# Where the rounded half of an FFN hidden block is read from, and which semaphore TensorE waits on for its bank

## The chip, the cores and the metric

The kernel runs on 1 core of a Trainium2 chip. The metric is device time of one execution in microseconds (us). Three runs of the kernel before took 3048.17, 3043.27 and 3048.67 us; their median is 3048.17 us.

## The reference

The reference is a stack of four residual sublayers over 32 independent sequences of 512 rows and 256 columns, all in fp32:

```
x = x + attn_a(layernorm(x))   # 16 heads, linear attention: phi = elu + 1, causal cumulative sums, numer / denom
x = x + ffn(layernorm(x))
x = x + attn_b(layernorm(x))   # 16 query heads on 4 kv heads, rotary, window of 64, softmax, pair mixing
x = x + ffn(layernorm(x))

def ffn(x):                    # W1: 1024 x 256, W2: 256 x 1024, both rounded to -1, 0, 1
    h = relu(x @ quantize(W1).T + b1)
    return h @ quantize(W2).T + b2
```

The change touches only the line of `h`.

## The kernel before

**Split numbers.** TensorE multiplies fp32r operands, which hold fewer bits than fp32. So each fp32 operand is kept as two fp32r halves: the rounded value and what is left over. For the FFN's hidden block these are `f_hh` (rounded, written by ScalarE) and `f_hl` (`f_r - f_hh`, written by VectorE, line 1314), where `f_r` is the relu in full fp32.

**One FFN turn.** A turn is one FFN over one sequence (512 rows): 8 blocks (`fb` 0 to 7) of 128 hidden units. `up(fb)` is four matmuls into a PSUM bank `HID` (line 439). ScalarE's `f_relu` (lines 969 to 976) reads that bank twice: once for `f_r`, once more for `f_hh`. VectorE's `low(fb)` makes `f_hl`. `down(fb)` adds eight matmuls into the banks `Y` (line 459). In the main loop all blocks use the one bank `HID[0]` (`ONE_HID`), so `up(fb+1)` has to wait until ScalarE is through with block `fb`.

**The order.** The order of work is written out by hand, one list for each engine. A step of the main loop has two phases. In phase 1 sequence `a` is in attention A, and an FFN of two other sequences is woven in; in phase 2 sequence `b` (the one before) is in attention B, again with FFN blocks between. Each phase runs blocks 5, 6, 7 of a carried turn and 0 to 4 of its own. So a step has 16 `f_relu`, one after another on ScalarE and in a fixed place of its queue. Each engine works through its own queue in order and waits on semaphores. All of this is unrolled in the program as `phase1` and `phase2` of each engine, and the middle steps are a hardware loop.

**Names that the prediction uses.** Start of phase 2 on TensorE: `up(5)`, `up(6)`, `down(4)`, `turn_q(0)` (line 744, waits for VectorE's `stack_lo(0)`, lines 1613 and 1614). On ScalarE: `relu(5)`, `raw(2)` (lines 1010, 1011, 1014), `stack_hi(0)` (lines 1133, 1134), `relu(6)`, `exps(0)` (line 1156). On VectorE, from the end of phase 1: `residual(3)` (line 1458), the roots (lines 1560 to 1583, each instruction waits for the one before by a semaphore of VectorE's own), `rotate` (line 1599), `stack_lo(0)`. On GpSimd: `sines` (lines 1805, 1806), released by `raw`. Later in phase 1: ScalarE's `relu(3)`, then `y_hi(2)` (line 1070), VectorE's `y_lo(2)` (line 1450), TensorE's `project(2)` (line 379). From phase 2 into phase 1: ScalarE's `relu(4)`, then `qk_exp(0)` (lines 1056, 1057); TensorE's `qk(2)` (line 379) waits for it. The start and the end of the program run an FFN by itself (`alone`).

**Semaphores.** `f_rr` counts finished `f_r`; `f_act` counts finished `f_hh`. Before the change nothing waits on `f_rr`.

Of the kernel before, what the change touches and what calls it, by code (L numbers as in the profile page):

```python
# [20 lines left out]
ACT = mybir.ActivationFunctionType  # L21
# [14 lines left out]
FB = FF // P  # L36
# [10 lines left out]
UPS, DOWNS = 5, 4  # L47
# [43 lines left out]
def needed(value):  # L91

    return not isinstance(value, int) or value > 0


def build(nc, x, w_qkv, w_out, w_b, wo_b, gain, mix, w1, b1, w2, b2, const, out):
    with ExitStack() as ctx:
        def sb(name, shape, dt=F32):
            return ctx.enter_context(nc.sbuf_tensor(name, shape, dt))

        def sem(name):
            return ctx.enter_context(nc.semaphore(name))
# [18 lines left out]
        b1c = sb("b1c", [P, FB])  # L121
# [15 lines left out]
        class Norm:  # L137
# [20 lines left out]
        f_r = sb("f_r", [P, 2, S])  # L158
        f_hh = sb("f_hh", [P, 2, S], F32R)
# [63 lines left out]
        f_h, f_rr, f_act, f_lo, f_w2, f_out = (sem(n) for n in (  # L223
            "f_hidden_ready", "f_relu_ready", "f_hi_ready", "f_lo_ready", "f_down_done", "f_added"))
# [46 lines left out]
        def first_turn(s):  # L271

            return None if s is None else 0 if isinstance(s, int) and s == 0 else s * 2 - 1

        def second_turn(s):

            return None if s is None else 2 * NSEQ - 1 if isinstance(s, int) and s == NSEQ - 1 else s * 2 + 2
# [85 lines left out]
        def _(pe):  # L363
# [19 lines left out]
            def norm_half(n, turn, hf, bank):  # L383
                pe.wait_ge(n.normed, turn * NT + 2 * hf + 2)
                for k in range(KB):
                    for t in range(2):
                        mm = pe.transpose(bank[:, k * D + t * P:k * D + (t + 1) * P],
                                          n.xn[:, 2 * hf + t, k * P:(k + 1) * P], ident)
                mm.then_inc(n.turned, 1)

            def norm_transpose(n, turn, banks):
                for hf in range(2):
                    norm_half(n, turn, hf, banks[hf])

            def at_half(turn, hf, own, carry):

                if turn is None:
                    return
                if hf:
                    pe.wait_ge(at.lo, turn * 2 + 1)  # L400
                elif own is not None:
                    pe.wait_ge(f_act, own * FB + 3)
                else:
                    pe.wait_ge(f_act, (carry + 1) * FB)
                norm_half(at, turn, hf, HID[0])

            def f_norm(turn):
                if needed(turn * FB):

                    pe.wait_ge(f_act, turn * FB)  # L410
                norm_transpose(ff, turn, HID)

            def f_half(turn, hf):

                if turn is None:
                    return
                if hf:
                    pe.wait_ge(ff.lo, turn * 2 + 1)
                elif needed(turn * FB):
                    pe.wait_ge(f_act, turn * FB)  # L420
                norm_half(ff, turn, hf, HID[0])

            def f_up(turn, fb, at_turn=None, banks=TWO_HID):

                if turn is None:
                    return
                if fb == 0:
                    pe.wait_ge(ff.lo, turn * 2 + 2)
                if fb == (UPS - 2 if banks is ONE_HID else UPS - 1) and at_turn is not None:

                    pe.wait_ge(at.lo, at_turn * 2 + 2)
                if banks is ONE_HID:
                    if fb:
                        pe.wait_ge(f_act, turn * FB + fb)
                elif fb >= 2:
                    pe.wait_ge(f_act, turn * FB + fb - 1)
                for k in range(KB):
                    for j, src in enumerate((ff.xh, ff.xl)):
                        mm = pe.matmul(banks[fb % 2][:], w1t[:, k, fb * P:(fb + 1) * P], src[:, k, :],  # L439
                                       start=(k == 0 and j == 0), stop=(k == KB - 1 and j == 1))  # L440
                mm.then_inc(f_h, 1)
# [22 lines left out]
            def f_unit(turn, k):  # L464
                if turn is not None:
                    if k + 1 < FB:
                        f_up(turn, k + 1)
                    if k >= 0:
                        f_down(turn, k)
# [5 lines left out]
            def alone(own, carry, last):  # L475

                for k in range(FB - DOWNS):
                    carried(carry, k)
                if own is not None:
                    f_norm(own)  # L480
                    for k in range(-1, FB if last else DOWNS):
                        f_unit(own, k)
# [39 lines left out]
            def program(guarded):  # L522
                def phase1(s):
                    a, n, own, carry = s.a, first_turn(s.a), second_turn(s.c), first_turn(s.b)
# [5 lines left out]
                    def up(fb):  # L530
                        f_up(own if fb < UPS else carry, fb, turn_b, ONE_HID)
# [4 lines left out]
                    def own_norm():  # L536
                        if own is not None:
                            f_norm(own)

                    def next_norm(half):  # L540
                        at_half(turn_b, half, own, carry)
# [25 lines left out]
                    def scores(ch):  # L567

                        if ch == 0:
                            pe.wait_ge(a_qz_s, (a + 1) * 4)  # L570
                            pe.wait_ge(a_ph, (a + 1) * 4)
                            pe.wait_ge(a_kt_s, (a + 1) * 2)
                            if own is not None:

                                pe.wait_ge(ff.lo, own * 2 + 2)
                            elif carry is not None:
                                pe.wait_ge(f_act, carry * FB + UPS)
                        else:

                            pe.wait_ge(a_sm, a * 16 + 4 * ch)  # L580
                            pe.wait_ge(a_ne, a * NT + ch)
                        for k in range(KB):
                            for r in range(4):
                                rows = slice(32 * r, 32 * r + 32)
                                mm = pe.matmul(A_SCORES[r][:, k * 2 * P:(k + 1) * 2 * P].rearrange("p (e q) -> p e q", e=2),  # L585
                                               a_kT[rows, k, ch * P:(ch + 1) * P], a_qz[rows, k, :, ch * P:(ch + 1) * P],
                                               start=(k == 0), stop=(k == KB - 1), skip_group_check=True)
                                if k == KB - 1:

                                    mm.then_inc(a_sc[r], 1)  # L590
# [78 lines left out]
                    down(6)  # L669
                    state(0)  # L670
                    scores(0)
                    up(0)
                    state(1)
# [4 lines left out]
                    up(1)  # L678
                    turn_numer(0)
                    scores(1)  # L680
                    up(2)
                    turn_y(0)
# [3 lines left out]
                    numer(1, 1)  # L686
                    turn_numer(1)
                    scores(2)
                    turn_y(1)
                    next_norm(0)  # L690
# [23 lines left out]
                def phase2(s):  # L714
# [5 lines left out]
                    def up(fb):  # L720
                        f_up(own if fb < UPS else carry, fb, turn_a, ONE_HID)
# [4 lines left out]
                    def own_norm(half):  # L726
                        f_half(own, half)

                    def next_norm(half):
                        at_half(turn_a, half, own, carry)  # L730
# [212 lines left out]
        def _(act):  # L943
# [25 lines left out]
            def f_relu(turn, fb, banks=TWO_HID):  # L969
                act.wait_ge(f_h, turn * FB + fb + 1)  # L970
                if needed(turn * FB + fb - 1):

                    act.wait_ge(f_lo, turn * FB + fb - 1)
                    act.wait_ge(f_w2, turn * FB + fb - 1)
                act.activation(f_r[:, fb % 2, :], banks[fb % 2][:], ACT.Relu, bias=b1c[:, fb:fb + 1]).then_inc(f_rr, 1)  # L975
                act.activation(f_hh[:, fb % 2, :], banks[fb % 2][:], ACT.Relu, bias=b1c[:, fb:fb + 1]).then_inc(f_act, 1)  # L976

            def alone(own, carry, last):
                if carry is not None:
                    for k in range(UPS, FB):  # L980
                        f_relu(carry, k)
                if own is not None:
                    f_norm(own)
                    for k in range(FB if last else UPS):
                        f_relu(own, k)
# [889 lines left out]
```

## Time and profile before

| | |
|---|---|
| median of 3 runs | 3048.17 us (3043.27 to 3048.67) |
| the profiled execution | 3042.93 us, its span 3041.1 us |
| TensorE busy | 2793.4 us, 92% of the span |
| VectorE busy | 2309.7 us, 76% |
| ScalarE busy | 1724.2 us, 57% |
| GpSimd busy | 475.7 us, 16% |
| mean granted TensorE clock | 0.986 of full speed |

In the rows further down, PE is TensorE's matmul row, PEld its weight loads, DVE VectorE, ACT ScalarE, POOL GpSimd. A timeline row begins with the start in us from the span's start and the duration in us. A duration reaches to the end of the instruction's last write; the next instruction of the same engine can start before that, so the spacing of two starts is shorter than a duration. Idle time of the engine just before an instruction stands in square brackets with what ended it; idle time under about 0.15 us is not printed. The share of busy time is an average over all stages.

### The profile page before, as it was taken

Reading aid. Unit: us, or ns where it says so; the run is one execution under the profiler, and the core shown is the slowest. Engines: PE = TensorE matmul, PEld = TensorE weight load, DVE = VectorE, ACT = ScalarE, POOL = GpSimd, SP = SyncE. Lnnn points to the kernel's source line nnn. Section 1 sums busy time; section 2 is a strip of 40 time slices with the busy share of each in tenths; the row PEclk is TensorE's granted clock in tenths of the full one; section 3 lists DMA queues with packets and bytes.
Section 4 is the critical chain, followed back from the end, with each engine's and each line's share of the span. In section 5 each row is a group of like instructions: output and inputs, shape, how many; then the busy total and the mean of one; then the engine's idle time right before and its main releaser. Section 6 shows DMA issues by size and latency. Waiting matters only on the chain. (4 is left out here: it accounts for less than half of the span.)

```text
span 3041.1 us, 75562 instructions
## 1 busy us (share of the span) xinstructions
PE 2793.4 (92%) x25924; PEld 2258.8 (74%) x25924; DVE 2309.7 (76%) x5982; ACT 1724.2 (57%) x3589; POOL 475.7 (16%) x1047
## 2 busy tenths in 40 slices
PE   5799999999999999999999999999999999999976
PEld 4577777777777777777777777777777777777764
DVE  6677787777788777788777788777788777788754
ACT  2356555566555566555566555566555556555554
POOL 4111111111111111111111111111111111111110
PEclk8999999999999999999999999999999999999998
DMA  2000000000000000000000000000000000000000
GB/s 69 8 11 17 16 16 3 14 16 16 16 16 3 14 16 16 16 16 7 9 16 16 16 16 9 7 16 16 16 16 10 6 16 16 16 16 11 6 11 17
DMA packets 42114, 45.10 MB, mean 15 GB/s; under 512 B 2640, under 2 KB 41424, under 8 KB 42064
## 3 DMA queue, kind: packets, MB, share of 16 engines
q1 hardware_dynamic: 42064, 44.46, 4.8%
q8 instruction: 28, 0.46, 0.1%
q14 instruction: 22, 0.18, 0.0%
HBM read 21.38 MB, written 16.78 MB: 13 GB/s over the span
## 5 line engine op out<-in xcount | busy, mean ns | idle before, releaser
L975 ACT ACTIVATE f_r<-HID,b1c 128x512 f32<-128x512 f32 x512 | 356.9, 697 | 520.4 <-PE HID L439 482.1
L459 PE MATMUL Y<-w2t,f_hh 128*128 128x256 f32 x2048 | 537.5, 296 | 6.3 <-DVE f_hl L1314 6.3
L459 PE MATMUL Y<-w2t,f_hl 128*128 128x256 f32 x2048 | 509.5, 281 | 0.0
L439 PE MATMUL HID<-ff_xh,w1t 128*128 128x512 f32 x1024 | 432.0, 422 | 69.5 <-ACT f_hh L976 43.5
L1314 DVE TENSOR_TENSOR f_hl<-f_r,f_hh 128x512 fp32r<-128x512 f32 x512 | 350.5, 685 | 114.6 <-ACT f_hh L976 110.1
L459 PEld LDWEIGHTS Y<-w2t,f_hh 128*128 128x128 f32 x2048 | 387.1, 189 | 35.4 <-issue 15.9
L439 PE MATMUL HID<-ff_xl,w1t 128*128 128x512 f32 x1024 | 406.9, 397 | 0.0
L459 PEld LDWEIGHTS Y<-w2t,f_hl 128*128 128x128 f32 x2048 | 388.3, 190 | 6.0
L976 ACT ACTIVATE f_hh<-HID,b1c 128x512 fp32r<-128x512 f32 x512 | 356.2, 696 | 0.0
L439 PEld LDWEIGHTS HID<-ff_xh,w1t 128*128 128x128 f32 x1024 | 193.8, 189 | 152.1 <-ACT f_hh L976 66.9
L1420 DVE TENSOR_TENSOR a_s<-Q,cst 128x512 f32<-128x512 f32 x384 | 246.3, 683 | 28.0 <-PE Q L585 28.0
L1156 ACT ACTIVATE a_qz<-Q 128x512 f32<-128x512 f32 x384 | 201.6, 603 | 47.9 <-PE Q L787 45.5
L439 PEld LDWEIGHTS HID<-ff_xl,w1t 128*128 128x128 f32 x1024 | 194.7, 190 | 23.7
L1064 ACT ACTIVATE a_relu<-Q 128x512 f32<-128x512 f32 x128 | 76.5, 598 | 200.2 <-PE Q L612 200.2
L1784 POOL TENSOR_SCALAR at_tmp<-at_mv 128x4 f32<-128x4 f32 x64 | 12.3, 193 | 1100.3 <-DVE at_mv L1292 1100.3
L1805 POOL TENSOR_TENSOR a_s<-a_s,cst 128x160 f32<-128x160 f32 x128 | 69.3, 541 | 666.5 <-ACT a_s L1011 660.7
L612 PE MATMUL Q<-a_s,a_v 128*32 128x128 f32 x4096 | 146.7, 278 | 3.1 <-DVE a_s L1420 2.9
L585 PE MATMUL Q<-a_qz,a_kT 32*128 32x256 f32 x1536 | 147.0, 403 | 2.0 <-DVE a_qz L1411 2.0
L1649 DVE TENSOR_TENSOR x<-Q,x 128x256 f32<-128x256 f32 x128 | 54.1, 423 | 121.7 <-PE Q L379 88.1
L585 PE MATMUL HID<-a_qz,a_kT 32*128 32x256 f32 x512 | 145.3, 403 | 0.0
L1070 ACT ACTIVATE a_yh<-Q 128x256 fp32r<-128x256 f32 x128 | 49.1, 384 | 167.4 <-PE Q L642 167.4
L1306 DVE TENSOR_TENSOR at_xl<-HID,at_xh 128x512 fp32r<-128x512 f32 x122 | 84.0, 689 | 56.4 <-ACT at_xh L960 56.4
(195 smaller groups left out, 7421.8 us busy)
## 6 DMA issues: line engine op xcount, KB each, us to landing
x<-in_x SPq DMA_DIRECT2D x32, 512.0 KB, 4.2
out<-x SPq DMA_DIRECT2D x32, 512.0 KB, 3.1
b_vm<-b_v SPq DMA_DIRECT2D x64, 96.0 KB, 2.2
x<-in_w SPq DMA_DIRECT2D x2, 512.0 KB, 4.1
a_s<-in_w_qkv SPq DMA_DIRECT2D x1, 768.0 KB, 5.1
cst<-in_const SPq DMA_DIRECT2D x1, 645.0 KB, 6.3
ff_xn<-in_w SPq DMA_DIRECT2D x1, 512.0 KB, 6.1
f_r<-in_w SPq DMA_DIRECT2D x1, 512.0 KB, 6.8
```

What stands on the lines that cost most here:

```text
L439: mm = pe.matmul(banks[fb % 2][:], w1t[:, k, fb * P:(fb + 1) * P], src[:, k, :], start=(k == 0 and j == 0), stop=(k == KB - 1 and j == 1))
L459: mm = pe.matmul(Y[t // 2][:, (t % 2) * D:(t % 2 + 1) * D], h[:, fb % 2, t * P:(t + 1) * P], w2t[:, fb, :], start=False, stop=(fb == FB - ...
L585: mm = pe.matmul(A_SCORES[r][:, k * 2 * P:(k + 1) * 2 * P].rearrange("p (e q) -> p e q", e=2), a_kT[rows, k, ch * P:(ch + 1) * P], a_qz[ro ...
L612: mm = pe.matmul(Q[3][VW * j:VW * (j + 1), cols], a_v[:, ch, k * HB + 2 * r + e, :], a_s[:, ch % 2, r, j * P:(j + 1) * P], start=(r == 0), ...
L975: act.activation(f_r[:, fb % 2, :], banks[fb % 2][:], ACT.Relu, bias=b1c[:, fb:fb + 1]).then_inc(f_rr, 1)
L976: act.activation(f_hh[:, fb % 2, :], banks[fb % 2][:], ACT.Relu, bias=b1c[:, fb:fb + 1]).then_inc(f_act, 1)
L1064: act.activation(a_nT, Q[3][:, :].rearrange("p (r q) -> p r q", r=4), ACT.Copy).then_inc(a_ne, 1)
L1156: act.activation(b_p[:, g, :], B_SCORES[g][:, :], ACT.Exp).then_inc(b_ex, 1)
L1306: dve.tensor_tensor(n.xl[:, :, hf * D:(hf + 1) * D], banks[hf][:, :].rearrange("p (k n) -> p k n", k=KB), n.xh[:, :, hf * D:(hf + 1) * D], ...
L1314: dve.tensor_tensor(f_hl[:, fb % 2, :], f_r[:, fb % 2, :], f_hh[:, fb % 2, :], ALU.subtract).then_inc(f_lo, 1)
L1420: dve.tensor_tensor(a_s[:, ch % 2, r, :].rearrange("p (h q) -> p h q", h=4), A_SCORES[r][:, :].rearrange("p (h q) -> p h q", h=4), causal. ...
L1805: pool.tensor_tensor(dst[:, :, 0:HD // 2], raw[:, :, HD // 2:], table("sin", t, 0, HD // 2), ALU.mult)
```

## The change

In `f_relu` the second ScalarE instruction becomes a plain copy of `f_r` in SBUF into `f_hh`, without a bias operand. It reads what the instruction ahead of it writes, so a wait for ScalarE's own `f_rr` stands between them. All waits of TensorE for `f_act` (six places, in `at_half`, `f_norm`, `f_half`, `f_up` and `scores`) become waits for `f_rr` with the same count. VectorE's wait in `low` stays on `f_act`. No instruction moves on any engine: each has the same instructions in the same order as before, one line further down from line 976 on.

```
                 elif own is not None:
-                    pe.wait_ge(f_act, own * FB + 3)
+                    pe.wait_ge(f_rr, own * FB + 3)
                 else:
-                    pe.wait_ge(f_act, (carry + 1) * FB)
+                    pe.wait_ge(f_rr, (carry + 1) * FB)
                 norm_half(at, turn, hf, HID[0])
...
                 if banks is ONE_HID:
                     if fb:
-                        pe.wait_ge(f_act, turn * FB + fb)
+                        pe.wait_ge(f_rr, turn * FB + fb)
                 elif fb >= 2:
-                    pe.wait_ge(f_act, turn * FB + fb - 1)
+                    pe.wait_ge(f_rr, turn * FB + fb - 1)
...
                 act.activation(f_r[:, fb % 2, :], banks[fb % 2][:], ACT.Relu, bias=b1c[:, fb:fb + 1]).then_inc(f_rr, 1)
-                act.activation(f_hh[:, fb % 2, :], banks[fb % 2][:], ACT.Relu, bias=b1c[:, fb:fb + 1]).then_inc(f_act, 1)
+                act.wait_ge(f_rr, turn * FB + fb + 1)
+                act.activation(f_hh[:, fb % 2, :], f_r[:, fb % 2, :], ACT.Copy).then_inc(f_act, 1)
```

## Rows read from the trace of the kernel before

**Rows 1.** The page's first part: engine, busy us, share of the span, instructions

```profile
PE 2793.4 (92%) x25924; PEld 2258.8 (74%) x25924; DVE 2309.7 (76%) x5982; ACT 1724.2 (57%) x3589; POOL 475.7 (16%) x1047
```

**Rows 2.** TensorE's waits: engine, line waited for: us in total, times, longest

```profile
PE HID L439 <- ACT f_hh L976: 43.5, 31, 2.9
...
PE Q L744 <- DVE b_ks L1614: 25.8, 60, 6.0
...
PE Y L459 <- DVE f_hl L1314: 6.3, 8, 3.5
```

**Rows 3.** Timeline of TensorE, start of phase 2 in one step

```profile
1519.78 0.50 PE L439 MATMUL HID<-ff_xh,w1t 128*128 128x512 f32 x1 [1.35 <-ACT f_hh L976]
...
1522.32 0.53 PE L744 MATMUL Q<-ident_r,b_qs 128*128 128x128 f32 x4 [0.40 <-DVE b_ks L1614]
```

**Rows 4.** Timeline of VectorE, same stretch and a later rotate

```profile
1515.50 0.18 DVE L1292 BATCH_NORM_AGGREGATE ff_mv<-ff_st 128x2 f32<-128x6 f32 x1 [0.15 <-DVE ff_st L1288]
...
1516.69 0.18 DVE L1562 TENSOR_SCALAR b_root<-b_var 128x20 int32<-128x20 int32 x1
1516.90 0.18 DVE L1565 TENSOR_TENSOR b_step<-b_root 128x20 f32<-128x20 f32 x1
...
1520.54 0.79 DVE L1599 TENSOR_TENSOR a_s<-a_s 128x320 f32<-128x320 f32 x1
...
1521.98 0.28 DVE L1614 TENSOR_TENSOR b_ks<-a_s,b_ks 128x128 fp32r<-128x128 f32 x1
...
1530.02 0.48 DVE L1599 TENSOR_TENSOR a_s<-a_s 128x320 f32<-128x320 f32 x1
```

**Rows 5.** Timeline of ScalarE, same stretch and on to exps(0)

```profile
1518.46 0.69 ACT L975 ACTIVATE f_r<-HID,b1c 128x512 f32<-128x512 f32 x1 [3.96 <-PE HID L439]
1519.05 0.68 ACT L976 ACTIVATE f_hh<-HID,b1c 128x512 fp32r<-128x512 f32 x1
1519.62 0.44 ACT L1010 ACTIVATE a_eq<-Q 128x320 f32<-128x320 f32 x1
...
1520.74 0.42 ACT L1133 ACTIVATE b_qs<-a_s 128x256 fp32r<-128x256 f32 x1 [0.24 <-DVE a_s L1608]
...
1524.21 0.70 ACT L976 ACTIVATE f_hh<-HID,b1c 128x512 fp32r<-128x512 f32 x1
1524.99 1.58 ACT L1156 ACTIVATE a_qz<-Q 128x512 f32<-128x512 f32 x3
```

**Rows 6.** ScalarE's groups by line and shape: xcount, busy us, mean ns

```profile
L976 ACT ACTIVATE f_hh<-HID,b1c 128x512 fp32r<-128x512 f32 x512 | 356.2, 696 | 0.0
...
L1046 ACT ACTIVATE a_kt<-Q 128x512 f32<-128x512 f32 x32 | 19.1, 598 | 0.0
```

**Rows 7.** Timeline of ScalarE at program start, two copies out of SBUF

```profile
21.43 0.63 ACT L952 ACTIVATE wout_h<-a_s 128x512 fp32r<-128x512 f32 x1 [2.20 <-DMA mixc<-in_mix]
21.97 0.83 ACT L953 ACTIVATE wb_h<-a_s 128x768 fp32r<-128x768 f32 x1
```

**Rows 8.** Timeline of GpSimd, start of phase 2, sines(2)

```profile
1520.46 0.52 POOL L1805 TENSOR_TENSOR a_s<-a_s,cst 128x160 f32<-128x160 f32 x1 [0.59 <-ACT a_s L1011]
```

**Rows 9.** Timeline of ScalarE, phase 2 into phase 1: relu(4), qk_exp(0)

```profile
1559.92 0.68 ACT L976 ACTIVATE f_hh<-HID,b1c 128x512 fp32r<-128x512 f32 x1
...
1560.97 0.61 ACT L1057 ACTIVATE a_relu<-Q 128x512 f32<-128x512 f32 x1
```

**Rows 10.** TensorE's weight loads, qk(2)

```profile
1561.62 0.19 PEld L379 LDWEIGHTS Q<-at_xh,wqkv_h 128*128 128x128 f32 x1 [0.19 <-ACT a_relu L1057]
```

**Rows 11.** Timeline of ScalarE in phase 1: relu(3), y_hi(2)

```profile
1506.78 0.68 ACT L976 ACTIVATE f_hh<-HID,b1c 128x512 fp32r<-128x512 f32 x1
1507.35 0.38 ACT L1070 ACTIVATE a_yh<-Q 128x256 fp32r<-128x256 f32 x1
```

**Rows 12.** Timeline of VectorE, y_lo(2)

```profile
1507.77 0.42 DVE L1450 TENSOR_TENSOR a_yl<-Q,a_yh 128x256 fp32r<-128x256 f32 x1
```

**Rows 13.** TensorE's weight loads, project(2)

```profile
1508.27 0.19 PEld L379 LDWEIGHTS Q<-wout_h,a_yh 128*128 128x128 f32 x1 [0.20 <-DVE a_yl L1450]
```

More of the change, by code:

```diff
@@ L408, in f_norm @@
                 if needed(turn * FB):
-                    pe.wait_ge(f_act, turn * FB)
+                    pe.wait_ge(f_rr, turn * FB)
                 norm_transpose(ff, turn, HID)
@@ L419, in f_half @@
                 elif needed(turn * FB):
-                    pe.wait_ge(f_act, turn * FB)
+                    pe.wait_ge(f_rr, turn * FB)
                 norm_half(ff, turn, hf, HID[0])
@@ L576, in scores @@
                             elif carry is not None:
-                                pe.wait_ge(f_act, carry * FB + UPS)
+                                pe.wait_ge(f_rr, carry * FB + UPS)
                         else:
```

## The prediction

> **What bounds the kernel now.** I read the page's shares first: TensorE is busy 92% of the span and ScalarE 57% [rows 1]. So ScalarE's total is not the question, but where ScalarE stands in TensorE's way. That is in the view of TensorE's waits, which the reader should take next: TensorE's matmul row idles on `f_hh` for 43.5 us, in 31 waits [rows 2]. That is one wait for each step of the loop and none at the other fifteen `up` of a step. The timeline of TensorE says which one: `up(6)` at the start of phase 2, which comes straight behind `up(5)` and sits 1.35 us until ScalarE has read the bank twice [rows 3]. It is 2.5 us later, in the same timeline, that TensorE waits again: `turn_q(0)` idles 0.40 us for VectorE's `stack_lo(0)` [rows 3]. The second row of [rows 2] is this wait, with that of `turn_q(1)`: 60 in all, two a step.
>
> So two chains run from the end of phase 1 to `turn_q(0)`: TensorE's own, with the `f_hh` wait in it, and VectorE's (residual, roots, rotate, `stack_lo`). VectorE's is the later one, by the 0.40 us.
>
> **What the change removes.** `f_r` starts at 1518.46 and takes 0.69, so it is done at 1519.15; `f_hh` is done at 1519.05 + 0.68 = 1519.73 [rows 5]. TensorE is let go at the first of these instead of the second, 0.58 us earlier. If all of it reached the end, that would be 31 x 0.58 = 18 us. I count it as nothing: `stack_lo(0)` ends at 1521.98 + 0.28 = 1522.26 whatever TensorE does, and `turn_q(0)` starts 0.06 us behind it [rows 3, 4]. TensorE then does `up(6)` and `down(4)` 0.58 us earlier and idles 0.98 instead of 0.40 us at `turn_q(0)`. The other waits that move to `f_rr` were not holding TensorE, by the count of 31.
>
> **What the change adds on ScalarE.** Today the second activation does not wait for the first: it starts 0.59 us behind it although the first takes 0.69 [rows 5]. The pair's `f_hh` is done 0.59 + 0.68 = 1.27 us after the pair's start, and the next instruction of the queue starts at 1519.62 - 1518.46 = 1.16 us [rows 5]. Now the copy reads what the relu writes, and waits for its end: 0.69, plus the time of the wait, plus the copy.
>
> The time of an own wait on ScalarE is in no row. On VectorE the chain of roots has such waits: one ends at 1516.69 + 0.18 = 1516.87 and the next starts at 1516.90, 0.03 us; the dearest own wait is 0.15 us [rows 4]. From ScalarE to VectorE it is 0.04 (1507.35 + 0.38 = 1507.73 to 1507.77) [rows 11, 12]. I take 0.04, for it is a plain wait on a count as in the roots, and keep 0.03 and 0.15 as ends.
>
> The copy's own time is in the trace, although in two instructions only: 128x512 from SBUF to fp32r takes 0.63 us, and the next starts 0.54 behind it [rows 7]. From PSUM without a bias it would be 0.60 [rows 6]; with the bias, as now, it is 0.68 to 0.70 [rows 5, 6].
>
> So `f_hh` is done at 0.69 + 0.04 + 0.63 = 1.36 us instead of 1.27 (0.09 later), and ScalarE's next instruction starts at 0.73 + 0.54 = 1.27 instead of 1.16 (0.11 later). With 0.03 and 0.15 the second number is 0.10 and 0.22.
>
> The Trainium skill ("ScalarE: Activation LUTs", What ACT_TABLE_LOAD costs) has a per-partition bias operand cost about 93 ns, and lets back-to-back activations overlap by about 93 ns. By that page the copy saves what the lost overlap costs, ScalarE is late by the wait alone, and the estimate for the sum below is 2 us in place of 7. The trace has the overlap at 0.10 us, and the copy from SBUF only 0.06 us shorter than the relu, not 0.09. A second page tells the memories apart: the Trainium skill ("Perfetto Trace Analysis", Optimizing Scalar/DVE Operations) gives ScalarE about 93 ns of access on SBUF and 51 on PSUM, and the rows have 0.63 and 0.60. This second rule speaks against moving the read to SBUF, and the rows side with it.
>
> **Where that 0.11 us lands.** In the timelines I went through the sixteen `f_relu` of a step and looked at what ScalarE, VectorE and TensorE do next. Mostly ScalarE idles behind the pair, or VectorE comes to the block later anyway. Three places remain, and one that is just covered.
>
> First, `relu(4)` at the end of phase 2. Behind its `f_hh` ScalarE runs `qk_exp(0)` without a pause; its relu ends at 1560.97 + 0.61 = 1561.58, and TensorE's weight load for `qk(2)`, which needs that bank, starts 0.04 us later after an idle 0.19 [rows 9, 10]. No slack: 0.11 us a step.
>
> Second, `relu(3)` in phase 1. `y_hi(2)` starts 0.57 behind `f_hh`, that is, as soon as the queue lets it; VectorE's `y_lo(2)` follows 0.04 behind and ends at 1508.19; `project(2)`'s weight load starts at 1508.27 [rows 11 to 13]. A wait costs TensorE 0.04 to 0.06 elsewhere in these rows, so 0.03 of the 0.08 is slack: 0.08 us a step.
>
> Third, `relu(5)` in phase 2, with `raw(2)` behind it, at 1519.62 [rows 5]. `stack_hi(0)` has an idle 0.24 in front of it that ends with VectorE [rows 5], so it takes the 0.11 and is not late. But `raw(2)` also releases GpSimd's `sines(2)`, which starts at 1520.46, just ahead of VectorE's `rotate` at 1520.54 [rows 4, 8]. That `rotate` takes 0.79, and 0.48 where GpSimd does nothing [rows 4]: the two hold each other up by 0.31. With `sines(2)` at 1520.57 it is the second of the two. `rotate` then gains up to 0.31, and the next pair of instructions, `sines(2)`'s second half and `stack_lo(0)`, meets instead. Bounds: -0.31 and +0.31 us a step on the chain that `turn_q(0)` waits for. I take +0.02: what one gains the other loses.
>
> The covered one: `exps(0)` starts 0.78 behind `f_hh` of `relu(6)`, held by TensorE's scores [rows 5]. The new pair needs 0.14 + 0.54 = 0.68. It hides with 0.10 to spare at a wait of 0.04; at 0.15 it comes 0.01 late.
>
> The program's start and end run FFN blocks by themselves, and there TensorE waits for `f_hl` eight times [rows 2]; each comes 0.09 later: 0.7 us.
>
> **Sum.** (0.11 + 0.08 + 0.02) x 31 = 6.5, and 0.7: 7.2 us more, less nothing. The profiled execution took 3042.93 us with a span of 3041.1, so it would take about 3050. That execution is 5.2 us under the median of the three runs (3048.17); set against the median the sum is 3055 us, which I predict.
>
> **Rivals.**
> *The removed wait does reach the end.* For it: it is the longest wait of TensorE, and 0.58 us of it go. It needs `stack_lo(0)` to be over 0.58 us earlier too, which only the `rotate` gain could help, by 0.31 at most. Against: 0.40 us of idle time behind `stack_lo(0)` in the step shown. With the 0.31 in full, 31 x 0.31 = 9.6 less the 6.6 of the other terms: 3045; with everything, 18 less 6.6: 3037. It decides from the point where `stack_lo(0)` gains more than 0.21 us.
> *No change.* The two pushes are swallowed: the copy is 0.03 to 0.04 shorter than the single early rows say, or a delay of TensorE there shortens a wait further on (the 0.40 us, the wait for `f_hl`). 3048, within 3. By the first page of the Trainium skill named above it would be this one.
> *The own wait is as dear as VectorE's dearest, 0.15.* Then 0.22 + 0.19 + 0.02 + 0.01 = 0.44 a step, and 1.6 us at the ends: 15 us, 3063. Against: the 0.15 stands at one kind of instruction, and the roots' own wait is at 0.03.
> *GpSimd gets in front of `stack_lo(0)`.* 0.31 x 31 = 9.6 on top of the 6.6: 3064. For it: in the pair shown, GpSimd's and VectorE's starts are 0.08 us apart [rows 4, 8]. Against: `stack_lo(0)` comes late in the stretch, when `sines(2)` is nearly over. The Trainium skill ("SBUF — State Buffer", Summary: rules for kernel authors) says that of VectorE with two SBUF inputs and GpSimd the second to issue is blocked until the first is through; the 0.31 agrees.
>
> **Chances and range.** My forecast (4 to 11 us more) 0.44; no change 0.28; the removed wait, 0.11; the dear own wait, 0.08; GpSimd in front, 0.09. What a measurement of this kernel can tell from no change is about 0.2%, 6.1 us. The forecast lies across that line: I give 0.28 of its 0.44 to slower and 0.16 to no change. Slower: 0.28 + 0.08 + 0.09 = 0.45. Same: 0.16 + 0.28 and 0.02 of the first rival = 0.46. Faster: 0.09. Range 3040 to 3068: from the first rival's middle to past the two dear cases. The forecast alone has 3050 to 3060, with the three runs' own spread of 5 us.
>
> **What would show it.** Right: TensorE's idle time before `up(6)` falls from 1.35 to about 0.8 and that before `turn_q(0)` grows from 0.40 to about 1.0. `f_hh` takes 0.63 and starts 0.04 behind the end of `f_r`. The weight loads of `qk(2)` and `project(2)` start 0.1 us later against the loads before them. The prediction is wrong if the idle time before `turn_q(0)` stays near 0.40, if the copy takes 0.60 or less, or if `rotate` falls to 0.48 and `stack_lo(0)` ends earlier against `residual(3)`.

## The result and the profile after

The changed kernel takes 3078.28 us (median of 6 runs, 3077.31 to 3083.04); the kernel before, run beside it, 3048.42 us (6 runs, 3043.27 to 3054.0). The ratio is 1.010, with a 95% interval of 1.0089 to 1.0110. So the change makes the kernel slower by 30 us, where I had predicted 3055 and a range that ended at 3068. The profiled execution of after took 3078.29 us, 35.4 us more than that of before.

The page's first part has the first sign. It answers to [rows 1]:

```profile
PE 2835.1 (92%) x25924; PEld 2293.6 (75%) x25924; DVE 2315.4 (75%) x5982; ACT 1754.2 (57%) x3589; POOL 476.6 (15%) x1047
```

TensorE runs the same 25924 matmuls, and is busy with them for 41.7 us more. An engine that only waits longer has more idle time, not more busy time. So its instructions themselves became longer. The costliest groups by line and shape (line, operation, tiles, count, busy us, mean ns) of before:

```profile
L459 PE MATMUL Y<-w2t,f_hh 128*128 128x256 f32 x2048 | 537.5, 296 | 6.3 <-DVE f_hl L1314 6.3
L459 PE MATMUL Y<-w2t,f_hl 128*128 128x256 f32 x2048 | 509.5, 281 | 0.0
```

and of after:

```profile
L459 PE MATMUL Y<-w2t,f_hh 128*128 128x256 f32 x2048 | 554.5, 302 | 6.2 <-DVE f_hl L1315 6.2
L459 PE MATMUL Y<-w2t,f_hl 128*128 128x256 f32 x2048 | 523.4, 287 | 0.0
```

`down` alone has 30.9 us of the 41.7. Its operands, shapes and count are unchanged, so what is left is the clock. The view of the cores (span, mean granted TensorE clock) of after says so:

```profile
core 0: 3076.5 us, clock 0.971
```

In before it is 0.986. Now to where it falls. TensorE's waits of after, which answer to [rows 2]:

```profile
PE Q L744 <- DVE b_ks L1615: 40.5, 37, 6.0
...
PE HID L439 <- ACT f_r L975: 25.6, 31, 2.3
...
PE Y L459 <- DVE f_hl L1315: 6.2, 8, 3.6
```

The wait of `up(6)` fell by 17.9 us and that of line 744 for `stack_lo` grew by 14.7. Its count fell from 60 to 37: `turn_q(0)` still waits in every step, and `turn_q(1)` no longer does in the 23 steps in which the clock falls (further down). TensorE's timeline of after, start of phase 2 in the same step as [rows 3]:

```profile
1535.21 0.50 PE L439 MATMUL HID<-ff_xh,w1t 128*128 128x512 f32 x1 [0.78 <-ACT f_r L975]
...
1536.26 0.28 PE L459 MATMUL Y<-w2t,f_hh 128*128 128x256 f32 x1
1536.38 0.28 PE L459 MATMUL Y<-w2t,f_hl 128*128 128x256 f32 x1
...
1538.40 0.54 PE L744 MATMUL Q<-ident_r,b_qs 128*128 128x128 f32 x4 [1.03 <-DVE b_ks L1615]
...
1539.91 0.37 PE L781 MATMUL Q<-hot,qfirst_rows 32*128 32x256 bf16 x3 [0.80 <-ACT b_kT L1148]
...
1542.30 0.41 PE L459 MATMUL Y<-w2t,f_hh 128*128 128x256 f32 x1
1542.51 0.41 PE L459 MATMUL Y<-w2t,f_hl 128*128 128x256 f32 x1
```

The idle time before `up(6)` and before `turn_q(0)` is 0.78 + 1.03 = 1.81 us, before it was 1.35 + 0.40 = 1.75: nearly the same in sum, but most of it now stands behind `down(4)` instead of ahead of `up(6)`. Then come only six small transposes, and another 0.80 us of idle time that was there before too (0.79). Behind it come the scores (lines 781 and 787, 1.8 us) and then `down(5)`, which runs at a spacing of 0.21 us; `down(4)`, some 5 us earlier, ran at 0.12. The same stretch as windows (length, busy time and count of PE, PEld, DVE, ACT, POOL, then PEclk):

```profile
1534.50:1540.00 5.50, 2.96 (x22) 2.43 (x26) 5.44 (x13) 4.45 (x13) 4.25 (x7) 1.00 0.08 20
1540.00:1543.40 3.40, 3.40 (x40) 3.04 (x39) 3.12 (x11) 2.61 (x6) 0.00 (x0) 0.50 0.10 25
1543.40:1550.00 6.60, 6.60 (x68) 5.15 (x67) 4.83 (x14) 4.47 (x11) 0.00 (x0) 1.00 0.00 0
```

For 3.4 us TensorE is granted 0.50, its lower level of 1.2 GHz, and is busy all through them; on either side it has 2.4 GHz. In before the same place has 1.00:

```profile
1524.00:1527.40 3.40, 3.27 (x52) 2.52 (x48) 3.13 (x11) 3.32 (x8) 0.00 (x0) 1.00 0.10 24
```

It is not so in every step. Windows of after from `turn_q(0)` on, 6.16 us each, in four neighbouring steps:

```profile
1630.84:1637.00 6.16, 5.37 (x54) 4.37 (x58) 4.88 (x16) 4.72 (x11) 1.23 (x2) 0.72 0.13 32
1723.58:1729.74 6.16, 5.08 (x68) 3.62 (x69) 5.69 (x19) 5.59 (x12) 1.22 (x2) 1.00 0.13 32
1814.84:1821.00 6.16, 5.37 (x54) 4.46 (x58) 5.02 (x16) 4.64 (x11) 1.23 (x2) 0.72 0.13 32
1907.17:1913.33 6.16, 5.36 (x54) 4.38 (x58) 4.88 (x16) 4.65 (x11) 1.22 (x2) 0.72 0.13 32
```

The second has no fall, although its idle times are the same (0.78, 1.03 and 0.79). I count a step from the start of `relu(5)` in one phase 2 to the next, over the 29 steps of full length. In before they take 2642.89 us and the clock never falls in them. In after they take 2673.31 us, and it falls in 23 of the 29: such a step takes 92.2 to 92.7 us (median 92.37), one without 91.3 to 91.5 (median 91.34), and the median step of before takes 91.13. So 30.4 of the 35.4 us are in the loop. The rest is at the ends, where executions of one kernel also differ by some us; what makes it up is not shown.

On ScalarE the pair is as the prediction had it. Its timeline of after, answering to [rows 5]:

```profile
1534.47 0.69 ACT L975 ACTIVATE f_r<-HID,b1c 128x512 f32<-128x512 f32 x1 [3.96 <-PE HID L439]
1535.19 0.63 ACT L977 ACTIVATE f_hh<-f_r 128x512 fp32r<-128x512 f32 x1
1535.73 0.42 ACT L1011 ACTIVATE a_eq<-Q 128x320 f32<-128x320 f32 x1
```

The own wait costs 1535.19 - (1534.47 + 0.69) = 0.03 us, the copy 0.63, and `raw(2)` starts 1.26 us behind the relu instead of 1.16.

### The profile page after: what moved, and what is told of

The parts are those of the page before. It is cut to its first block and busy times, and to the rows that moved or that the text cites. A ratio compares the mean times of both kernels' runs of the same rounds, so it can differ in the third digit from the quotient of the medians.

```text
span 3076.5 us, 75562 instructions
## 1 busy us (share of the span) xinstructions
PE 2835.1 (92%) x25924; PEld 2293.6 (75%) x25924; DVE 2315.4 (75%) x5982; ACT 1754.2 (57%) x3589; POOL 476.6 (15%) x1047
## 5 line engine op out<-in xcount | busy, mean ns | idle before, releaser
L459 PE MATMUL Y<-w2t,f_hh 128*128 128x256 f32 x2048 | 554.5, 302 | 6.2 <-DVE f_hl L1315 6.2
L459 PE MATMUL Y<-w2t,f_hl 128*128 128x256 f32 x2048 | 523.4, 287 | 0.0
L459 PEld LDWEIGHTS Y<-w2t,f_hh 128*128 128x128 f32 x2048 | 399.7, 195 | 37.5 <-issue 20.8
L459 PEld LDWEIGHTS Y<-w2t,f_hl 128*128 128x128 f32 x2048 | 401.4, 196 | 5.9
L977 ACT ACTIVATE f_hh<-f_r 128x512 fp32r<-128x512 f32 x512 | 323.4, 632 | 16.3
L1806 POOL TENSOR_TENSOR a_s<-a_s,cst 128x160 f32<-128x160 f32 x128 | 80.7, 630 | 666.7 <-ACT a_s L1012 660.9
L744 PEld LDWEIGHTS Q<-ident_r,b_qs 128*128 128x128 f32 x512 | 51.4, 142 | 112.0 <-issue 64.4
```

What stands on the lines that cost most here:

```text
L459: mm = pe.matmul(Y[t // 2][:, (t % 2) * D:(t % 2 + 1) * D], h[:, fb % 2, t * P:(t + 1) * P], w2t[:, fb, :], start=False, stop=(fb == FB - ...
L977: act.activation(f_hh[:, fb % 2, :], f_r[:, fb % 2, :], ACT.Copy).then_inc(f_act, 1)
L1806: pool.tensor_tensor(dst[:, :, 0:HD // 2], raw[:, :, HD // 2:], table("sin", t, 0, HD // 2), ALU.mult)
```

## The experiments

The theory: the change delays ScalarE a little (4 to 7 us in all), and the larger part, some 26 us, is the clock, which falls because TensorE's idle time has moved from the front of `up(6)` to the front of `turn_q(0)`, with only six small transposes between it and the 0.80 us behind them. The rivals: the copy or its wait costs the 30 us itself, with the clock as a mere companion; or it is `f_rr` that lets something collide. All "step" figures are medians over the 29 steps of the profiled execution; "falls" are steps of the 29 in which the granted clock goes to 0.50. Each ratio is against the kernel before as it ran beside the experiment: 3047.70 us (25 runs) for the first four, 3049.22 (16 runs) for the copy at three places and for the first three with `sines(1)` early, 3046.61 (21 runs) for the copy at two places and for the last.

**The copy alone.** The kernel before with the last two lines of the change only:

```
+                act.wait_ge(f_rr, turn * FB + fb + 1)
+                act.activation(f_hh[:, fb % 2, :], f_r[:, fb % 2, :], ACT.Copy).then_inc(f_act, 1)
```

> The copy and its own wait alone; all of TensorE's waits stay on f_act. Clock theory (the removed wait moved TensorE's idle time to one place, where the granted clock then falls to 1.2 GHz in about 20 of 31 steps, some 22 us; ScalarE's lateness costs the other 7 to 8): about 3056 us, mean granted clock back at 0.985, no fall in the main loop. Rival (ScalarE's lateness of 0.1 us in each pair costs all 30 us): about 3078 us, as the changed kernel.

Measured: 3054.12 us (10 runs), ratio 1.0025 (1.0016 to 1.0035). The clock falls in no step, and a step takes 91.27 us. TensorE's timeline:

```profile
1526.35 0.50 PE L439 MATMUL HID<-ff_xh,w1t 128*128 128x512 f32 x1 [1.44 <-ACT f_hh L977]
1528.86 0.54 PE L744 MATMUL Q<-ident_r,b_qs 128*128 128x128 f32 x4 [0.38 <-DVE b_ks L1615]
```

So the copy with its wait costs 6.4 us by the medians (5 to 11 by the interval), 0.14 us a step in the loop. The other 24 us come with the moved waits.

**One wait moved back.** The changed kernel, in which `up(6)` of phase 2 alone waits for `f_act`:

```
-                        f_up(own if fb < UPS else carry, fb, turn_a, ONE_HID)
+                        f_up(own if fb < UPS else carry, fb, turn_a, ONE_HID, f_act if fb == 6 else f_rr)
```

> The changed kernel, with the one wait of up(6) in phase 2 back on f_act; all others on f_rr. Clock theory: up(6) idles 1.4 us again and turn_q(0) about 0.4, the clock holds, about 3056 us, the same as the copy alone. Rival that ScalarE's lateness costs it all: 3078. Rival that several of the moved waits matter: between the two.

Measured: 3055.31 us (10 runs), ratio 1.0027 (1.0017 to 1.0036), no fall, step 91.27. TensorE's timeline:

```profile
1521.65 0.50 PE L439 MATMUL HID<-ff_xh,w1t 128*128 128x512 f32 x1 [1.44 <-ACT f_hh L977]
1524.18 0.54 PE L744 MATMUL Q<-ident_r,b_qs 128*128 128x128 f32 x4 [0.39 <-DVE b_ks L1615]
```

That is the copy alone again. All that was lost beyond the copy hangs on one wait of a step; the others that moved to `f_rr` make no difference clear of the noise (3055.31 against 3054.12). The change moves seven waits in the text of the kernel, not six as I had counted.

**The idle time filled.** The changed kernel with three spare matmuls ahead of `turn_q(0)`; they go into a bank that is overwritten, nothing reads them, and ahead of them stands a wait that `turn_q(0)` has too:

```
                     down(4)
+                    fill(3)      # 3 x pe.matmul(Q[2], w1t[:, 0, 0:P], ff.xh[:, 0, :])
                     turn_q(0)
```

> The changed kernel with three more matmuls of 128x512 (results overwritten, nothing reads them) on TensorE between down(4) and turn_q(0), some 0.7 us in the idle 1.03. Clock theory: no fall of the clock in the main loop, about 3056 us although TensorE does more. Rival that ScalarE's lateness costs it all: 3078 or more. Rival that TensorE lacks time there: 3078 + 31 x up to 0.7 = 3100.

Measured: 3055.74 us (10 runs), ratio 1.0023 (1.0013 to 1.0034), no fall, step 91.27. TensorE's timeline (L735 are the spare ones, L749 is `turn_q(0)`):

```profile
1524.72 0.50 PE L439 MATMUL HID<-ff_xh,w1t 128*128 128x512 f32 x1 [0.78 <-ACT f_r L981]
...
1526.71 0.86 PE L735 MATMUL Q<-ff_xh,w1t 128*128 128x512 f32 x3
1527.91 0.54 PE L749 MATMUL Q<-ident_r,b_qs 128*128 128x128 f32 x4 [0.34 <-DVE b_ks L1621]
```

`up(6)` is as early as in after, `turn_q(0)` as late as in the copy alone, and 22.5 us of the loss are gone by useless work. This is the strongest run for the clock: the wait on `f_rr` is there, and so are all other effects that it could have. (The last of the 29 steps takes 1.2 us longer than the others with the spare matmuls; why is not shown.)

**The idle time put together without the change.** The kernel before, with two entries of TensorE's list exchanged:

```
                     up(5)
-                    up(6)
                     down(4)
+                    up(6)
                     turn_q(0)
```

> The kernel before, ScalarE and all waits untouched; at the start of phase 2 TensorE runs down(4) ahead of up(6) instead of behind it. up(6) then no longer waits, and the 1.35 us join the 0.40 at turn_q(0). Clock theory: the clock falls in most steps as in the changed kernel, 3048 + (20 to 31) x 1.1 = 3070 to 3082. Rival that ScalarE's lateness is the cause: 3048, no change, since turn_q(0) is held by VectorE as before.

Measured: 3075.17 us (4 runs), ratio 1.0099 (1.0080 to 1.0118), falls in 29 of 29 steps, step 92.14. TensorE's timeline, then windows of it, with PEclk third from the end:

```profile
1534.86 0.50 PE L439 MATMUL HID<-ff_xh,w1t 128*128 128x512 f32 x1 [0.41 <-ACT f_hh L976]
...
1537.38 0.53 PE L744 MATMUL Q<-ident_r,b_qs 128*128 128x128 f32 x4 [1.32 <-DVE b_ks L1614]
```

```profile
1533.60:1539.75 6.15, 3.62 (x50) 2.72 (x48) 5.98 (x16) 5.15 (x14) 4.09 (x7) 1.00 0.13 32
1539.75:1543.15 3.40, 3.40 (x20) 2.88 (x16) 3.07 (x10) 2.79 (x7) 0.00 (x0) 0.51 0.00 0
```

ScalarE's work and every semaphore are those of before, the sum of the idle time is 1.73 us as before, and the loss of after is there: 1.0 us a step. The fall needs neither the copy nor `f_rr`. What this kernel has in common with after is the long idle time at `turn_q(0)`.

**The copy one place later.** The changed kernel with the spare matmuls, and `f_hh` put behind the next instruction of ScalarE's queue at the prediction's three places (behind `y_hi(2)`, `qk_exp(0)` and `raw(2)`), for instance

```
-                    relu(5)
+                    relu(5, True)          # f_r only
                     if s.a is not None:
                         raw(b, 2)
+                    round_of(5)            # f_hh
```

> The filler kernel (the changed one with three spare matmuls ahead of turn_q(0), clock held), and in three places of a step the copy into f_hh stands one place further down ScalarE's queue: behind y_hi(2), behind raw(2), behind qk_exp(0). ScalarE then has nothing to wait for in between. If those three places are where ScalarE's lateness costs (0.14 us a step in the copy-alone run), the loop's step goes from 91.27 back to 91.13 us and the time from 3055.7 to about 3051. Rival, that f_hh itself being late is what costs (VectorE and down wait for it): no gain, 3055 or more, since f_hh comes later still in these places.

Measured: 3058.68 us (5 runs), ratio 1.0036 (1.0022 to 1.0051), 3 falls, step 91.40. I had expected about 3051, or 3055 by the rival: it is no better than without, and a step is 0.13 us longer. VectorE's timeline tells why:

```profile
1529.62 0.79 DVE L1635 TENSOR_TENSOR a_s<-a_s,b_rs 128x320 f32<-128x320 f32 x1
1530.33 0.79 DVE L1626 TENSOR_TENSOR a_s<-a_s 128x320 f32<-128x320 f32 x1
```

With `raw(2)` earlier GpSimd's `sines(2)` (1529.36 to 1530.78) runs beside these two instructions of VectorE, which both take 0.79 us, where without the deferring they take 0.48. `turn_q(0)` is 0.25 us later, TensorE's idle time there is back at 0.59, and in three steps the clock falls.

**At two places only,** `qk_exp(0)` and `y_hi(2)`, the rest as in the run above:

> The changed kernel with the three spare matmuls ahead of turn_q(0), and the copy put one place later in ScalarE's queue at two places only: behind y_hi(2) and behind qk_exp(0), not behind raw(2). Theory (ScalarE's lateness at qk(2) and project(2) makes the last 0.14 us of a step; the third deferral cost the previous version 0.25 us at turn_q(0)): step 91.1 us, no fall of the clock in the loop, 3048 to 3052. Rival (deferring does nothing at these two places, since f_hl comes later instead): step 91.27 as with the spare matmuls alone, 3055.

Measured: 3049.79 us (11 runs), ratio 1.0010 (1.0001 to 1.0019), no fall, step 91.19. So 0.08 of the 0.14 us a step were at these two places, and deferring gives them back; if `f_hl` comes later for it, that costs less than the deferring wins. The 0.08 make some 2.5 us over the 29 steps (2648.55 to 2646.07); the rest of the 5.9 us between the two medians lies outside the loop and is not explained.

**VectorE's chain shortened.** Four kernels have `sines(1)` ahead of `own_rstd` on GpSimd, so that it doesn't meet VectorE's rotate:

```
                     sines(0)
+                    sines(1)
                     own_rstd()
-                    sines(1)
```

First the kernel before with this edit:

> The kernel before, with GpSimd's sines(1) ahead of own_rstd instead of behind it: it then runs 4 us earlier, where VectorE has single-input work, and no longer beside rotate(0) and cosines(1). Theory that VectorE's chain is what ends last at turn_q(0): it gets up to 0.43 us shorter (0.12 at rotate(0), 0.30 at cosines(1)), turn_q(0) loses its 0.40 us idle, up to 31 x 0.40 = 12 us: 3036 to 3042. Rival, that TensorE's wait at up(6) bounds this stretch: 3048, no change.

Measured: 3031.58 us (4 runs), ratio 0.9948 (0.9932 to 0.9965), no fall, step 90.74. That is a larger gain than the 3036 to 3042 that I had expected. VectorE's timeline (the first is rotate, 0.60 us in before; the second took 0.78):

```profile
1514.30 0.48 DVE L1599 TENSOR_TENSOR a_s<-a_s 128x320 f32<-128x320 f32 x1
1514.70 0.48 DVE L1592 TENSOR_TENSOR a_s<-a_s,cst 128x320 f32<-128x320 f32 x1
```

and TensorE's, where `turn_q(0)` has no idle time left that the view prints:

```profile
1515.15 0.50 PE L439 MATMUL HID<-ff_xh,w1t 128*128 128x512 f32 x1 [1.35 <-ACT f_hh L976]
...
1517.01 0.28 PE L459 MATMUL Y<-w2t,f_hl 128*128 128x256 f32 x1
1517.35 0.53 PE L744 MATMUL Q<-ident_r,b_qs 128*128 128x128 f32 x4
```

and the end of `stack_lo(0)` on VectorE:

```profile
1517.02 0.28 DVE L1614 TENSOR_TENSOR b_ks<-a_s,b_ks 128x128 fp32r<-128x128 f32 x1
```

This is what a removed wait on the bounding chain brings: 0.39 us a step. It beats both kernels. The two chains now end together: `down(4)` at 1517.01 + 0.28 = 1517.29, `stack_lo(0)` at 1517.02 + 0.28 = 1517.30. Then the changed kernel with it:

> The changed kernel with sines(1) ahead of own_rstd. The removed wait at up(6) can pay only when VectorE's chain is shorter. Clock theory: TensorE idles 0.6 instead of 1.0 us at turn_q(0), and if that is enough for the clock to hold all through the loop, the time is the one of the kernel before with the same move, plus 4: about 3042. If the clock still falls in some steps, 3042 + 1.1 for each. Rival that the change in itself slows TensorE: 3078 less 12, 3066.

Measured: 3058.18 us (10 runs, 3047 to 3069), ratio 1.0036 (1.0021 to 1.0051), 16 falls; a step without one takes 90.9 us, with one 92.0. The executions differ by the clock: the shortest, 3047.30 us, has a mean granted clock of 0.983, the longest, 3068.77 us, one of 0.972. The idle time at `turn_q(0)` is 0.70 us in both kinds of step, for instance

```profile
1528.15 0.54 PE L744 MATMUL Q<-ident_r,b_qs 128*128 128x128 f32 x4 [0.70 <-DVE b_ks L1615]
```

The same with the three deferrals:

> The changed kernel with sines(1) ahead of own_rstd and the copy one place further down in the three places; no spare matmuls. With both, raw(2) and stack_hi(0) come up to 0.57 us earlier on ScalarE too, so VectorE's chain can end up to 0.6 us earlier than before and the removed wait pays: 3030 to 3040, if the clock holds. If ScalarE's place does not matter: as the run without the deferral.

Measured: 3038.04 us (6 runs), ratio 0.9967 (0.9955 to 0.9980), 1 fall, step 90.61, idle time 0.56. From 1.32 us (29 falls) over 1.03 (23) and 0.70 (16) to 0.56 (1) the falls follow the idle time at `turn_q(0)`, although these four kernels differ in other things too. The step is 0.13 us under that of the kernel before with `sines(1)` early. Of this, 0.07 us are at `turn_q(0)`, which comes 3.44 us behind `relu(5)` instead of 3.51: `raw(2)` no longer stands behind `f_hh`, and with `sines(1)` out of the way that does VectorE no harm. The rest would be at the two other places; no run separates it. The whole time is no better: in the profiled executions the 29 steps take 2630.5 us against 2632.4, but what lies outside them 404.5 against 397.0. Last, the spare matmuls and the two deferrals with it:

> The same, with sines(1) ahead of own_rstd on GpSimd as well. Theory (VectorE's chain bounds turn_q(0), the clock is held by the spare matmuls): step 90.6 to 90.7 us, no fall, 3031 to 3036, no better than the kernel before with sines(1) early (3031.6), since what the change takes off TensorE's wait is given back at turn_q(0). Rival (with VectorE's chain shortened by 0.35 us the removed wait reaches the end): step 90.4 us or less, 3025 or less.

Measured: 3040.47 us (11 runs), ratio 0.9983 (0.9974 to 0.9992), no fall, step 90.79 against the 90.74 of the kernel before with `sines(1)` early. The rival's 90.4 or less is not reached, and neither are the 3031 to 3036 that I had expected; again the larger part of the gap is outside the 29 steps (402.7 us against 397.0). TensorE now reaches `turn_q(0)` as VectorE is through: the spare matmuls take up the 0.58 us, so this run alone could not have shown a gain. But in the changed kernel with `sines(1)` early and no spare matmuls `turn_q(0)` comes 3.58 us behind `relu(5)` too, after 0.70 us of idle time. So VectorE's chain still ends last there, and the wait removed at `up(6)` gives nothing. Whether it would with a still shorter chain, no run shows.

## Why the prediction was wrong

**The removed wait: right in its mechanism, wrong in its price.** I counted it at nothing, since `stack_lo(0)` holds `turn_q(0)`: "TensorE then does `up(6)` and `down(4)` 0.58 us earlier and idles 0.98 instead of 0.40 us at `turn_q(0)`." It idles 1.03. The step that failed is the one that priced that idle time at zero. I had treated idle time in front of a bounding wait as free wherever it stands, and here it cost the granted clock of what came behind. The missing term is 23 falls. Each is 1.03 us by the steps with and without one (92.37 - 91.34), or 1.13 by the whole loop (30.4 us less the 4.5 of the copy alone, over 23): 24 to 26 us. None of my rivals had it: I read the granted clock as a mean of 0.986, and did not ask what keeps it at 1.00 in this stretch.

The Trainium skill ("TensorE: Matmul & The Clock Gate", A second HAM failure mode: psum-queue depth-cycling) tells of a kernel in which short idle times between groups of matmuls let the clock go up and down. This trace agrees as far as that goes, with 0.78, 1.03 and 0.80 us of idle time ahead of a stretch at 0.50; but 1.35, 0.40 and 0.79 us in before, nearly the same in sum, let it stay at 1.00.

**ScalarE's lateness: right in kind, and too large by half for the step.** The pair came as predicted (0.03 against 0.04 for the wait, 0.63 for the copy, 1.26 against 1.27 to the next instruction). Per step it cost 0.14 us (91.27 - 91.13) instead of 0.21. At `qk(2)` and `project(2)` TensorE's weight loads of after show it, answering to [rows 10, 13]:

```profile
1578.90 0.19 PEld L379 LDWEIGHTS Q<-at_xh,wqkv_h 128*128 128x128 f32 x1 [0.27 <-ACT a_relu L1058]
```

```profile
1524.28 0.19 PEld L379 LDWEIGHTS Q<-wout_h,a_yh 128*128 128x128 f32 x1 [0.26 <-DVE a_yl L1451]
```

That is 0.08 and 0.06 us more, where I had 0.11 and 0.08, and not all of it reaches the end of the step: by the run with the copy at two places later they cost 0.08 us together. The copy alone cost 6.4 us by the medians, and my sum was 7.2. That these are so close is in part luck, for the 29 steps have only 4.5 of it, and the rest is outside them, where I had 0.7. Had the clock stayed, some 3055 would have been the time; the two runs with nearly all of the change but no fall (one wait moved back; the spare matmuls) have 3055.3 and 3055.7.

**The third place: right in kind.** I had said that what rotate gains `stack_lo(0)` loses. VectorE's timeline of before has, beside the rotate of 0.79 in [rows 4],

```profile
1521.65 0.41 DVE L1613 TENSOR_TENSOR b_qs<-a_s,b_qs 128x256 fp32r<-128x256 f32 x1
```

and that of after

```profile
1536.57 0.48 DVE L1600 TENSOR_TENSOR a_s<-a_s 128x320 f32<-128x320 f32 x1
...
1537.41 0.73 DVE L1614 TENSOR_TENSOR b_qs<-a_s,b_qs 128x256 fp32r<-128x256 f32 x1
```

They take 1.20 us together before and 1.21 after. GpSimd's `sines(2)` of after, answering to [rows 8]:

```profile
1536.55 0.86 POOL L1806 TENSOR_TENSOR a_s<-a_s,cst 128x160 f32<-128x160 f32 x1 [0.65 <-ACT a_s L1012]
1537.37 0.49 POOL L1807 TENSOR_TENSOR a_s<-a_s,cst 128x160 f32<-128x160 f32 x1
```

Its first half takes 0.86 instead of 0.52: of this pair it is now GpSimd's instruction that is held up. I had it start behind `rotate` for that; by these rows it still starts first, by 0.02 us instead of 0.08, but GpSimd's times in the profile are rough. In the copy alone `turn_q(0)` comes 3.92 us behind `relu(5)` instead of 3.86: 0.06 us, where I had 0.02.

**The rivals.** The removed wait pays: no. With VectorE's chain 0.35 us shorter the two chains of the kernel before end together, and of the changed kernel VectorE's still ends last, with 0.70 us of idle time at `turn_q(0)`. No change: no, since the copy alone costs 0.14 us a step. The dear own wait: no, since it takes 0.03 us. GpSimd in front of `stack_lo(0)`: not by the change (0.41 to 0.73 is paid for by rotate). But its 0.31 was real: the run that moved `sines(1)` out of VectorE's way gained 0.39 us a step, the run that moved `sines(2)` into it lost 0.25 us at `turn_q(0)`.

**What stays open.** Why 6 of the 29 steps of after keep 2.4 GHz with the same idle times, and from which idle time on the clock falls. The runs only order it. They also do not separate the length of the idle time at `turn_q(0)` from its place beside the 0.80 us behind the transposes.

## What to carry to other kernels

A wait that is taken off an engine ahead of a later, bounding wait is not removed but moved there; ask what stands around its new place. On TensorE, the same idle time may cost nothing in one place and the granted clock in another: here 1.35 us ahead of twelve dense matmuls (`up(6)` and `down(4)`) left it at 1.00 in all 29 steps, and 1.03 us behind them, six small transposes away from another 0.80, went with a fall in 23 of 29. So read the granted clock of that stretch, not its mean over the span, and treat 1.00 beside idle time as something that a change can lose. When TensorE's busy time grows at an unchanged count of matmuls, look at the clock first.

## What the runs showed of the hardware

An idle time of 1.03 instead of 0.40 us ahead of six small transposes and another 0.80, with 0.06 us more of it in sum, came with a fall of TensorE from 2.4 to 1.2 GHz for 3.4 us in 23 of 29 steps, at 1.0 to 1.1 us each; three matmuls that nothing reads (0.86 us) held it at 2.4 GHz. On ScalarE an own wait costs 0.03 us itself, and the 0.10 us by which two instructions otherwise overlap. A 128x512 copy from SBUF takes 0.63 us (632 ns in the mean of all 512). Where an instruction of VectorE and one of GpSimd meet in SBUF, one of the two is held up, and which one can change: in before VectorE's `rotate` took 0.79 instead of 0.48 us, in after GpSimd's half of `sines(2)` 0.86 instead of 0.52, and then VectorE's part of `stack_lo(0)` 0.73 instead of 0.41.
